# Attention with a fused 1x1 convolution on one core: the output turned by VectorE in 32x32 squares instead of by TensorE

## The reference

```python
xf = x.reshape(b, c, n)                                   # 4, 256, 4096
q = jnp.einsum('oc,bcn->bon', Wq, xf) + bq[None, :, None] # 32 rows
k = jnp.einsum('oc,bcn->bon', Wk, xf) + bk[None, :, None]
v = jnp.einsum('oc,bcn->bon', Wv, xf) + bv[None, :, None] # 256 rows
att = jax.nn.softmax(jnp.einsum('bdi,bdj->bij', q, k) / sqrt(32), axis=-1)
out = gamma * jnp.einsum('bcj,bij->bci', v, att).reshape(b, c, h, w)
cat = jnp.concatenate([out, x], axis=1)
fused = jnp.einsum('oc,bchw->bohw', Wf, cat) + bf[None, :, None, None]
```

## Time and profile before

| | |
|---|---|
| median of 3 runs | 2033.83 us (2033.78 to 2034.09) |
| profiled execution, its own time | 2033.3 us |
| its span, first to last instruction | 2031.4 us |
| PE busy | 2015.3 us, 99% |
| ACT busy | 1748.9 us, 86% |
| DVE busy | 1584.9 us, 78% |
| POOL busy | 1206.1 us, 59% |
| granted TensorE clock | 1.000 of full speed |
| transfers, mean share of the 16 DMA engines | 10% |

### The profile page before, as it was taken

How to read it: one execution, slowest core, us unless ns; L and a number is a source line. 1 busy time by engine, 2 the same in 40 slices (tenths; PEclk the granted TensorE clock), 3 DMA queues, 4 the chain that set the end, 5 groups by cost and what they waited for, 6 DMA issues and landing times.

```text
span 2031.4 us, 45017 instructions
## 1 busy us (share of the span) xinstructions
PE 2015.3 (99%) x16232; PEld 1980.4 (97%) x16232; DVE 1584.9 (78%) x2157; ACT 1748.9 (86%) x2373; POOL 1206.1 (59%) x514
## 2 busy tenths in 40 slices
PE   9999999999999999999999999999999999999999
PEld 8999999999899999999989999999998999999999
DVE  6788888886778888888677888888867788888885
ACT  7888888887888888888788888888878888888886
POOL 0467766667056677666605666766660666677665
PEclk9999999999999999999999999999999999999999
DMA  4200000000310000000031000000003100000000
GB/s 136 84 22 22 15 15 21 21 21 12 120 70 22 22 21 15 16 21 21 11 125 65 22 21 21 21 10 21 21 11 130 38 22 21 21 21 18 13 21 17
DMA packets 54081, 69.46 MB, mean 34 GB/s; under 512 B 4048, under 2 KB 37584, under 8 KB 53968
## 3 DMA queue, kind: packets, MB, share of 16 engines
q1 hardware_dynamic: 53696, 67.91, 10.0%
q10 hardware_dynamic: 272, 0.07, 0.0%
HBM read 34.41 MB, written 33.55 MB: 33 GB/s over the span
## 4 chain that ended last, share of the span: by engine, by line
PE 92%; DVE 3%; ACT 3%; issue 2%; DMA 0%; DVEq 0%; ACTq 0%; SPq 0%
PE ps_o L388 72%; PE ps_s L380 11%; PE ps_p L242 3%; PE ps_o L242 2%; PE ps_t L284 1%; ACT queries L478 1%; ACT hi L453 1%; DVE val_lo L676 1%; PE ps_s L259 1%; PE ps_t L276 1%; PE ps_t L269 1%; DVE top L612 1%; DVE lo L599 1%; PE ps_t L242 0%; DVE raw L626 0%
## 5 line engine op out<-in xcount | busy, mean ns | idle before, releaser
L755 POOL TENSOR_TENSOR raw<-raw,top_m 128x1024 f32<-128x1024 f32 x508 | 1205.4, 2413 | 809.1 <-ACT top_m L464 809.1
L631 DVE TENSOR_TENSOR lo<-ps_p,hi 128x1024 fp32r<-128x1024 f32 x512 | 626.9, 1224 | 311.4 <-ACT ps_p L545 311.1
L612 DVE TENSOR_TENSOR top<-ps_s,top 128x512 f32<-128x512 f32 x960 | 660.0, 687 | 55.6 <-ACT raw L459 7.4
L538 ACT ACTIVATE hi<-raw 128x1024 fp32r<-128x1024 f32 x512 | 543.9, 1062 | 145.9 <-PE ps_o L388 141.4
L388 PE MATMUL ps_o<-val_hi,hi 128*128 128x258 f32 x4096 | 664.5, 284 | 4.1 <-ACT hi L538 4.1
L388 PE MATMUL ps_o<-val_lo,hi 128*128 128x256 f32 x4096 | 652.4, 281 | 0.0
L459 ACT ACTIVATE raw<-ps_s 128x512 f32<-128x512 f32 x1024 | 554.1, 595 | 54.7 <-PE ps_s L380 32.0
L388 PE MATMUL ps_o<-val_hi,lo 128*128 128x258 f32 x4096 | 599.3, 284 | 0.0
L388 PEld LDWEIGHTS ps_o<-val_hi,hi 128*128 128x128 f32 x4096 | 562.4, 189 | 5.8 <-issue 4.6
L388 PEld LDWEIGHTS ps_o<-val_lo,hi 128*128 128x128 f32 x4096 | 560.4, 189 | 0.0
L388 PEld LDWEIGHTS ps_o<-val_hi,lo 128*128 128x128 f32 x4096 | 538.7, 190 | 0.0
(11 more groups left out here) (72 smaller groups left out, 1028.3 us busy)
## 6 DMA issues: line engine op xcount, KB each, us to landing
xf<-x SPq DMA_DIRECT2D x32, 512.0 KB, 3.7
conv_d<-conv_st SPq DMA_DIRECT2D x64, 256.0 KB, 2.0
result<-conv_d SPq DMA_DIRECT2D x64, 256.0 KB, 2.6
out<-result SPq DMA_DIRECT2D x64, 256.0 KB, 2.2
raw<-wf2T SPq DMA_DIRECT2D x1, 256.0 KB, 3.9
raw<-wv SPq DMA_DIRECT2D x1, 256.0 KB, 4.3
raw<-wf1T SPq DMA_DIRECT2D x1, 256.0 KB, 4.7
raw<-wkqT ACTq DMA_DIRECT2D x1, 64.0 KB, 2.0
```

What stands on the lines that cost most here:

```text
L538: nc.scalar.activation(hi[:, t % 2], raw[:, slot].rearrange("p j i -> p (j i)"), ACT.Exp, scale=SCALE).then_inc(hi_done, 1)
L612: nc.vector.tensor_tensor(top[:, new], scores, top[:, new if half else old], ALU.max).then_inc(max_done, 1)
L631: nc.vector.tensor_tensor(lo[:, t % 2], ps_p[:].rearrange("p h n -> p (h n)"), hi[:, t % 2].bitcast(F32), ALU.subtract).then_inc(lo_done, 1)
L755: nc.gpsimd.tensor_tensor(raw[:, slot], raw[:, slot], top_m[:, r].unsqueeze(1).broadcast_to((P, JQ, I)), ALU.subtract).then_inc(sub_done, 1)
```

## The change

The four PE transposes of a block are taken out. DVE turns `o_norm` in 32x32 squares instead, in one instruction (`nc.vector.transpose`, L648 of the changed kernel) from SBUF to a new SBUF tile `o_turn`. Such a transpose leaves each square in the group of 32 partitions in which it was: partition 32g + q of `o_turn` then holds, for each channel 32c + q and each of the two 128-query tiles i, the 32 queries i*128 + 32g to i*128 + 32g + 31. `result` has the same layout. POOL, in place of DVE, adds the convolution half, in its quad t = 4. Because a partition group now holds one stretch of 32 queries, the load and the store of a block are each cut into 8 transfers (2 tiles x 4 partition groups), each of 32 partitions x 8 channels x 32 queries, in runs of 128 bytes. In the kernel before each was one transfer of 128 partitions x 2 x 256 queries, in runs of 1024 bytes. PE no longer waits for `finished` ahead of `turn_top` or ahead of the convolution of chunk 0.

```diff
-    out_v = out.rearrange("b (k p) n -> b p k n", p=P)
+    out_v = out.rearrange("b (c q) n -> b q c n", q=SQ)
+    conv_q = conv_d.rearrange("b (c q) n -> b q c n", q=SQ)
...
-        result = sb("result", [P, OUTS, KT, I], F32)
+        result = sb("result", [P, OUTS, CT, IT * SQ], F32)
+        o_turn = sb("o_turn", [P, CT, IT, SQ], F32)
...
             def load_conv(b, n):
-                sp.dma_start(result[:, n % OUTS], conv_v[bass.ds(b, 1), :, :, n * I:(n + 1) * I].rearrange(
-                    "b p k n -> p (b k) n")).then_inc(conv_loaded[n % OUTS], 16)
+                for i in range(IT):
+                    for g in range(GROUPS):
+                        at = n * I + i * P + g * SQ
+                        sp.dma_start(result[g * SQ:(g + 1) * SQ, n % OUTS, :, i * SQ:(i + 1) * SQ], conv_q[
+                            bass.ds(b, 1), :, :, at:at + SQ].rearrange(
+                            "b q c n -> q (b c) n")).then_inc(conv_loaded[n % OUTS], 16)
...
             def store(b, n):
                 sp.wait_ge(finished, b * BLOCKS + (n + 1))
-                sp.dma_start(out_v[bass.ds(b, 1), :, :, n * I:(n + 1) * I].rearrange("b p k n -> p (b k) n"),
-                             result[:, n % OUTS]).then_inc(stored[n % OUTS], 16)
+                for i in range(IT):
+                    for g in range(GROUPS):
+                        at = n * I + i * P + g * SQ
+                        sp.dma_start(out_v[bass.ds(b, 1), :, :, at:at + SQ].rearrange("b q c n -> q (b c) n"),
+                                     result[g * SQ:(g + 1) * SQ, n % OUTS, :, i * SQ:(i + 1) * SQ]).then_inc(
+                                         stored[n % OUTS], 16)
...
-            def turn_out(B):
-                pe.wait_ge(o_scaled, B * IT)
-                for i in range(IT):
-                    for k in range(KT):
-                        last = nc.tensor.transpose(ps_t[:, k * I + i * P:k * I + (i + 1) * P],
-                                                   o_norm[:, i, k * P:(k + 1) * P], ident[:])
-                last.then_inc(o_turned, 1)
...
-            def add_conv(B, r, loaded):
-                dve.wait_ge(o_turned, B + 1)
-                dve.wait_ge(conv_loaded[r], loaded)
-                nc.vector.tensor_tensor(result[:, r], ps_t[:].rearrange("p (k n) -> p k n", k=KT), result[:, r],
-                                        ALU.add).then_inc(finished, 1)
+            def turn_out(B):
+                dve.wait_ge(o_scaled, (B + 1) * IT)
+                nc.vector.transpose(o_turn[:], o_norm[:].rearrange("p i (c q) -> p c i q", q=SQ)).then_inc(o_turned, 1)
...
+            def add_conv(B, r, loaded):
+                pool.wait_ge(o_turned, B + 1)
+                pool.wait_ge(conv_loaded[r], loaded)
+                nc.gpsimd.tensor_tensor(result[:, r], o_turn[:].rearrange("p c i q -> p c (i q)"), result[:, r],
+                                        ALU.add).then_inc(finished, 1)
...
+                    if t == 4 and not (isinstance(n, int) and n == 0):
+                        before = (r + OUTS - 1) % OUTS
+                        use = (n - 1) // OUTS if isinstance(n, int) else (n - 1 - before) // OUTS
+                        add_conv(B - 1, before, b * (LANDED * IT * USES[before]) + (use * (LANDED * IT) + LANDED * IT))
```

More of the change, by code:

```diff
@@ L35, in attention_conv @@
     R3 = 3 * CK
+    SQ = 32
+    GROUPS = P // SQ
+    CT = C_IN // SQ
+    LANDED = 16 * GROUPS
     SCALE = float(CK) ** -0.5
@@ L200, in _ @@
             for i in range(OUTS):
-                sp.sem_inc(stored[i], 16)
+                sp.sem_inc(stored[i], LANDED * IT)
             load_x(0, 0)
@@ L213, in _ @@
             for i in range(OUTS):
[L214 removed]
+                sp.wait_ge(stored[i], IMAGES * (LANDED * IT * USES[i]) + LANDED * IT)
         @block.tensor
@@ L261, in scores, with turn_top @@
                     last.then_inc(s_ready, 1)
-            def turn_top(B, done):
-                if done is not None:
-                    pe.wait_ge(finished, done)
+            def turn_top(B):
                 pe.wait_ge(top_j_done, B + 1)
@@ L320, in project @@
                         project_values(j)
-                    turn_top(b * BLOCKS, None)
+                    turn_top(b * BLOCKS)
                     pe.wait_ge(q_out, C + 1)
@@ L340, in project @@
                 if finishing:
-                    turn_out(b * BLOCKS)
+                    pe.wait_ge(o_scaled, b * (BLOCKS * IT) - 1)
                 project_values(0)
@@ L344, in project @@
                 if not start:
[L345 to L348, removed]
+                    pe.wait_ge(conv_done, C * 2)
                     convolve(ps_t[:], 0)
+                if finishing:
+                    pe.wait_ge(o_scaled, b * (BLOCKS * IT))
                 project_values(2)
@@ L425, in attend @@
                         lead(t, 1)
-                        if t == 1 and not first:
-                            pe.wait_ge(m_done, B + 1)
-                            turn_out(B)
                         if t == 5 and not last_block:
@@ L435, in attend @@
                         if t == 4 and not last_block:
[L436 to L441, removed]
+                            turn_top(B + 1)
+            images(pe, project, attend, lambda b: None)
         @block.scalar
@@ L721, in attend @@
                     if t == 2 and not first:
-                        before = (r + OUTS - 1) % OUTS
-                        use = (n - 1) // OUTS if isinstance(n, int) else (n - 1 - before) // OUTS
-                        add_conv(B - 1, before, b * (16 * USES[before]) + (use * 16 + 16))
+                        turn_out(B - 1)
                     if t == 4 and not last_block:
@@ L756, in subtract_top, with finish_image @@
                                         ALU.subtract).then_inc(sub_done, 1)
+            def add_conv(B, r, loaded):
[3 more added lines that the diff above has]
+                                        ALU.add).then_inc(finished, 1)
+            def finish_image(b):
+                add_conv(b * BLOCKS - 1, 0, b * (LANDED * IT * USES[0]))
             def project(b, c, first):
+                if c == 0 and not first:
+                    finish_image(b)
                 if c == CHUNKS - 1:
@@ L775, in attend @@
                         subtract_top((r + 1) % OUTS, slot)
-            images(pool, project, attend, lambda b: None)
+            images(pool, project, attend, finish_image)
 def kernel(**inputs):
```

7 lines of the change are left out of this document (3 added, 4 removed).

## The result

The changed kernel takes **2010.37 us** (median of 4 runs, 2010.15 to 2011.02); the kernel before, on the same chip, 2033.93. The ratio is 0.9885, 95% interval 0.987 to 0.9899: 23.6 us faster. Forecast were 2011.0. The profiled execution after took 2010.52 us with a span of 2008.0.

The account below looks back on a forecast made before the run. The prediction took PE, busy 2015.3 of 2031.4 us, to bound the kernel. From 2033.3 it took 27.7 for PE's transposes, added 0.6 for image starts and 4.3 for the tail, plus 0.5 for the median: 2011.0 us, range 2006.5 to 2022.

Parts of the forecast that it names:

- PE's transposes: Four transposes leave PE's chain at 63 visits, in blocks and image starts, 0.44 us each: 27.7 us less.
- DVE's transpose: One DVE instruction per block replaces DVE's addition: 0.68 us, between 0.34 and 1.2, hidden in DVE's 0.57 us wait.
- above some 3.5 us each further us costs 60 us: Limit for DVE's transpose time in a block: beyond it PE's low-part matmuls come late; a 4 us transpose gives 2041.
- POOL's addition: In each block POOL adds the convolution half in 1.2 us, bounds 0.7 and 2.4, at no cost.
- 4.5 us are left: POOL's spare time in a block after its addition, before ACT wants the subtractions of quads 6 and 7.
- the prediction's own room for x: At an image's start, chunk 2 of x landed 4.4 us before ACT took it in the kernel before.
- The packets: Each block's loads and stores: 35 ns per 128-byte packet, bounds 17 and 46, 4.8 us per store, hidden in blocks.
- The rival of slow packets: 128-byte packets read and written back, 92 ns each, delay image starts and the end: 2041.8 us; chance 12 in 100.
- The image start: Chunk 2 of x, issued behind the last store, lands 0.2 us late at three image starts: 0.6 us more.
- The tail: From the last o_norm's end to the span's end: 8.4 us instead of 4.06, so 4.3 us more.
- The sum: Whole kernel: 2033.3 - 27.7 + 0.6 + 4.3 = 2010.5 us against the profiled execution, 2011.0 for the median.

Follow-up runs that it names:

- experiment 1: Changed kernel with four unread 128x128 PE transposes put back in quad t = 1 of every block but an image's first: 2036.75 us.
- experiment 8: Changed kernel with two spare DVE transposes into a spare tile ahead of the real one in each block: 2045.3 us, ratio 1.0053 against the kernel before.
- experiment 9: Changed kernel with two spare DVE transposes behind the real one in each block: 2009.88 us.
- experiment 7: Changed kernel with three spare POOL additions of 128x512 ahead of the real one in each block: 2078.41 us, ratio 1.0219 against the kernel before.
- experiment 11: Kernel of experiment 6 with DVE's addition moved to t = 5 (t = 7 in an image's last block), where POOL has no subtraction under way: 2009.42 us.
- experiment 6: Changed kernel with the convolution half added by DVE in t = 2, right behind its transpose, POOL only subtracting: 2085.79 us, ratio 1.0248 against the kernel before.
- experiment 10: Changed kernel with three spare POOL additions behind each block's last subtraction: 2022.42 us, ratio 0.9942 against the kernel before.
- experiment 3: Changed kernel with each block's store issued twice, the second time to a spare tensor in device memory: 2031.92 us.

## Why the prediction was right, and where it was not

**PE's transposes: right.** Forecast -27.7, found -27.3 by the length of the blocks, and 26.4 for 60 blocks in experiment 1. The chain's 0.44 us was the price; the view by groups alone would have given 38.4. ACT let PE have it, as read from its 0.54 us of waiting.

**DVE's transpose: right size, wrong room.** 0.68 forecast, 0.70 found. But "above some 3.5 us each further us costs 60 us" failed. That bound looked at the engines that wait for DVE, and not at what a later `o_turn` pushes along on POOL. 1.3 us ahead of the real transpose cost 35 us (experiment 8); the same 1.3 behind it nothing (experiment 9).

**POOL's addition: right size, wrong room.** 1.2 forecast, 1.30 found, and nothing lost. "4.5 us are left" failed. I measured the room to ACT's need of quads 6 and 7. The first to feel POOL is DVE's `top_j`, which no semaphore ties to POOL, and there between -0.20 and +0.03 us were left inside the images. The trace of before could have told: I had POOL end at 423.4, and `top_j` at 423.86, 0.4 earlier in the changed kernel, starts at that very time. That it costs nothing is a touching fit and no reserve, and so it was luck. 3.8 us more on POOL cost 46 us in the blocks and 18 at the image starts, where the prediction's own room for x was used up (experiment 7).

**The packets: right side, wrong size.** I took 35 ns with bounds 17 and 46; it was 12.2, under the lower bound. I chose nearer to the 1024-byte row, because that was a store, though the two rows showed that a packet's price falls with its length. The rival of slow packets, with 12 in 100, fell: 77 ns were needed.

**The image start: x late by 0.6 us in all forecast, never late found,** for two reasons, packets that took 12 ns and issues of 0.47 us (3.77 / 8) instead of 0.53.

**The tail: +4.3 forecast, +3.4 found.** From `o_norm`'s end to the first issue it took 2.1 us, as forecast. From there seven issues took 3.3 us instead of 3.7, and from the start of the last one, at 2005.9, to the end it was 2.1 us and not 2.6. These two make the 0.9 us; why the last piece ends sooner was not tried (it is of 32 KB where the old store was of 256).

**The sum.** Against the profiled execution I forecast -22.8 and it was -22.8, by terms that cancel: 0.4 less gain in the blocks and 1.1 us that I had not counted (0.1 at the program's start, 0.4 at the second image's, 0.6 outside the span), against 0.9 too much for the tail and 0.6 for the image starts. That the parts are right to within a microsecond each is the reading; that their sum is right to a tenth is luck. The median then came 0.6 under the forecast, since I had added 0.5 for the median of the runs and this kernel's median lies 0.15 below its profiled execution.

## What to carry to other kernels

Price work taken off the bounding engine by the chain, not by busy time, and then see who ends last in that stretch: here both gave the blocks' part within half a microsecond. When an operand moves from PSUM to SBUF, or an instruction moves to POOL, list every DVE instruction with two SBUF operands that will run beside a POOL instruction, for this wait hangs on no semaphore and its room has to be read from start times. Small transfers in a loop can be free. They are not where a transfer that someone waits for stands behind them on the same queue (here x, at an image's start), nor at the program's end, where nothing covers their issue; there the old form may be kept for the last block alone.

## What was not expected of the hardware

- A DVE addition with two SBUF inputs takes 0.68 us where POOL is idle (experiment 11) and 2.54 in the mean among POOL's subtractions (experiment 6). DVE's transpose, with one SBUF input, was never held: in experiment 11 POOL subtracts from 403.30 to 415.18 us, and the transpose at 411.88 takes 0.70. All 64 take 0.70 to 0.71, and 60 of them lie wholly within one subtraction.
- Who starts first decides, down to 0.04 us (experiment 10), and it can be POOL that waits (experiment 6).
- 128-byte runs between SBUF and device memory: 12.2 ns of a DMA engine per packet in loads and stores together, where 1024-byte runs took 46. By bytes they are still dearer, 98 ns per 1024 bytes. Stores in such runs add nothing to what is read from device memory (34.41 MB with and without them).
- SP issues eight small transfers of 32 KB in 3.77 us, 0.47 each. At an image's end, beside packets of kind "instruction", one single issue took 1.82 us (experiment 3).

What stays open: whether the long issues at an image's end are waits for program code, and why PE's weight load idles 0.4 us longer at the second image's first block; neither was tried.
